# A decoder layer on one core: moments and normalisation of the next expert tokens placed in the group ahead, and routing in 20 steps

## The reference, cut to what matters

```python
scores = sigmoid(x @ gate_w.T);  scores_c = scores + correction_bias
group_scores = sum(top_k(scores_c.reshape(N, 4, 2), 2)[0], -1)
group_mask = one for the 2 best groups, else 0
scores_for_choice = where(repeat(group_mask, 2) > 0.5, scores_c, 0.0)
topk_idx = top_k(scores_for_choice, 4)[1]
topk_w = take_along_axis(scores, topk_idx);  topk_w = 2.5 * topk_w / (sum(topk_w) + 1e-20)
cw = topk_w scattered to the 8 experts
y_e = (silu(x @ Wg_e) * (x @ Wu_e)) @ Wd_e          # each expert, x is layernorm(x2)
out = x2 + sum_e cw_e * y_e + shared expert
```

## Time and profile before

| | |
|---|---|
| time, median of 3 runs (us) | 671.16 (670.51 to 671.90) |
| the profiled execution (us) | 671.73, of which the span is 669.9 |
| busy, share of the span | PE 97%, PEld 83%, DVE 72%, ACT 51%, POOL 37% |
| granted TensorE clock | 1.00 throughout, the 2.4 GHz level |
| expert stage | from 389.9 to 669.9, seven groups |

### The profile page before, as it was taken

How to read it: one execution, slowest core, us unless ns; L and a number is a source line. 1 busy time by engine, 2 the same in 40 slices (tenths; PEclk the granted TensorE clock), 3 DMA queues, 4 the chain that set the end, 5 groups by cost and what they waited for, 6 DMA issues and landing times. The chain is left out here.

```text
span 669.9 us, 11734 instructions
## 1 busy us (share of the span) xinstructions
PE 651.4 (97%) x3848; PEld 554.5 (83%) x3848; DVE 484.3 (72%) x1263; ACT 341.9 (51%) x794; POOL 248.7 (37%) x321
## 2 busy tenths in 40 slices
PE   5999999999999999999999989999999999999997
PEld 3868978888789788897887877888888888888887
DVE  5688778868788788787887978766767666667433
ACT  4555665667556666676576454343423434333321
POOL 2136365172463642624653132323233232332232
PEclk9999999999999999999999999999999999999999
DMA  7625134043150340522633180413204132140300
GB/s 203 168 57 156 36 101 139 0 136 102 53 158 27 107 131 0 159 79 63 189 93 100 49 269 1 158 64 127 94 3 159 60 126 94 28 162 1 135 24 32
DMA packets 51806, 64.44 MB, mean 96 GB/s; under 512 B 3944, under 2 KB 49560, under 8 KB 50880
## 3 DMA queue, kind: packets, MB, share of 16 engines
q1 hardware_dynamic: 51776, 64.06, 31.4%
HBM read 56.60 MB, written 7.45 MB: 96 GB/s over the span
## 5 line engine op out<-in xcount | busy, mean ns | idle before, releaser
L1593 POOL TENSOR_TENSOR xt<-xt,cw_wide 128x512 f32<-128x512 f32 x55 | 73.4, 1334 | 173.9 <-ACT xt L1550 173.9
L1617 DVE TENSOR_TENSOR res<-bank,xt 128x512 f32<-128x512 f32 x62 | 42.6, 687 | 53.1 <-POOL xt L1593 47.4
L1554 ACT ACTIVATE a_hi<-res 128x512 fp32r<-128x512 f32 x42 | 26.6, 634 | 86.5 <-DVE res L1617 86.5
L75 PE MATMUL bank<-h_hi,w_lo 128*128 128x512 f32 x168 | 67.4, 401 | 0.1
L77 PE MATMUL bank<-h_hi,w_hi 128*128 128x512 f32 x168 | 66.1, 393 | 0.0
L76 PE MATMUL bank<-h_lo,w_hi 128*128 128x512 f32 x168 | 66.0, 393 | 0.0
L75 PE MATMUL bank<-w_hi,op_lo 128*128 128x256 f32 x184 | 53.3, 290 | 0.5 <-DVE op_lo L1130 0.5
L76 PE MATMUL bank<-w_lo,op_hi 128*128 128x256 f32 x184 | 51.4, 280 | 0.0
L77 PE MATMUL bank<-w_hi,op_hi 128*128 128x256 f32 x184 | 51.4, 279 | 0.0
L1007 POOL TENSOR_TENSOR wz_lo<-tmp,wz_hi 128x512 fp32r<-128x512 f32 x28 | 35.0, 1281 | 37.6 <-DVE tmp L1173 37.6
L1622 DVE TENSOR_TENSOR a_lo<-res,a_hi 128x512 fp32r<-128x512 f32 x42 | 32.6, 776 | 22.4 <-ACT a_hi L1554 22.4
(11 more groups left out here) (239 smaller groups left out, 2059.8 us busy)
## 6 DMA issues: line engine op xcount, KB each, us to landing
cw_wide<-in_ctx_t SPq DMA_DIRECT2D x32, 375.0 KB
ctxf<-in_ctx SPq DMA_DIRECT2D x32, 375.0 KB
cw_wide<-cw_scratch SPq DMA_DIRECT2D x7, 1536.0 KB, 7.8
xt<-in_x SPq DMA_DIRECT2D x8, 448.0 KB, 4.1
x_scratch<-x2b SPq DMA_DIRECT2D x8, 448.0 KB, 3.2
x2n<-x_scratch SPq DMA_DIRECT2D x7, 512.0 KB, 4.7
cw_wide<-cw_scratch SPq DMA_DIRECT2D x7, 512.0 KB, 4.4
x2t<-x_scratch SPq DMA_DIRECT2D x7, 512.0 KB, 4.0
```

The source lines that it names most:

```text
L75: pe.matmul(dst, a_lo, b_hi, start=first, stop=False, **kw)
L1554: act.activation(a_hi[n % (AHEAD + 1)][:, :], af[(p + n) % 2][:, :], ACT.Copy).then_inc(a_hi_ok, 1)
L1593: pool.tensor_tensor(sg[b][:, :], sg[b][:, :], cw_wide[p][:, ORDER[n], :], ALU.mult).then_inc(sgw_ok, 1)
L1617: dve.tensor_tensor(af[b][:, :], u_bank[b][:, :], sg[b][:, :], ALU.mult).then_inc(af_ok, 1)
```

## The change

The change does two things.

**The norm moves ahead by most of a group.** `moments3`, `rstd3` and `normalise3` for group g + 2 now stand in group g: on DVE the moments after `act_low` 6 and the normalisation after `act_low` 7, on POOL rstd3 between expert 6 and expert 7. They are gone from the start of a group. Groups 0 to 4 do this (`more`).

**Routing in 20 steps.** Three pairs of a comparison or scaling and a product become one scalar_tensor_tensor each: choice, wsel and cw. The tile gmask is gone.

```diff
-            step(dve.tensor_scalar(gmask[:, :, :], grank[:, :, :], 2.0, None, ALU.is_lt))
-            step(dve.tensor_tensor(choice[:, :, :].rearrange("p t (a b) -> p t a b", b=2), halves,
-                                   gmask[:, :, :].unsqueeze(3).to_broadcast([P, T, 4, 2]), ALU.mult))
+            step(dve.scalar_tensor_tensor(choice[:, :, :].rearrange("p t (a b) -> p t a b", b=2),
+                                          grank[:, :, :].unsqueeze(3).to_broadcast([P, T, 4, 2]), 2.0, halves, ALU.is_lt, ALU.mult))
...
-            step(dve.tensor_scalar(erank[:, :, :], erank[:, :, :], 4.0, None, ALU.is_lt))
-            step(dve.tensor_tensor(wsel[:, :, :], score[:, :, :], erank[:, :, :], ALU.mult))
+            step(dve.scalar_tensor_tensor(wsel[:, :, :], erank[:, :, :], 4.0, score[:, :, :], ALU.is_lt, ALU.mult))
...
-            step(dve.tensor_tensor(wsel[:, :, :], wsel[:, :, :], winv[:, :].unsqueeze(2).to_broadcast([P, T, NEXP]), ALU.mult))
-            step(dve.tensor_scalar(cw[:, :, :], wsel[:, :, :], EXPERT_SCALE, None, ALU.mult))
+            step(dve.scalar_tensor_tensor(cw[:, :, :], winv[:, :].unsqueeze(2).to_broadcast([P, T, NEXP]), EXPERT_SCALE, wsel[:, :, :],
+                                          ALU.mult, ALU.mult))
...
@@ POOL, group @@
-                    if not last and not is_first(g):
-                        rstd3(pool, g + 1)
                     for n in range(2 if is_first(g) else 1, NE):
                         expert(g, p, n)
+                        if n == 6 and more:
+                            rstd3(pool, g + 2)
@@ DVE, group @@
-                    if not last and not is_first(g):
-                        moments3(dve, g + 1)
...
-                            if n == 0 and not is_first(g):
-                                normalise3(dve, g + 1)
                         if not is_first(g) or n >= 1:
                             act_low(g, p, n)
+                        if n == 6 and more:
+                            moments3(dve, g + 2)
+                        if n == 7 and more:
+                            normalise3(dve, g + 2)
```

More of the change, by code:

```diff
@@ L124, in decoder_layer @@
         lg, den, score, scorec, choice, wsel, cw = (osb(n, [P, T, NEXP]) for n in ("lg", "den", "score", "scorec", "choice", "wsel", "cw"))
-        gsum, grank, gmask = (osb(n, [P, T, 4]) for n in ("gsum", "grank", "gmask"))
+        gsum, grank = (osb(n, [P, T, 4]) for n in ("gsum", "grank"))
         g_gt, g_eq = osb("g_gt", [P, T, 4, 4]), osb("g_eq", [P, T, 4, 4])
@@ L144, in decoder_layer @@
         sg_ok, sgw_ok, af_ok, a_hi_ok, a_lo_ok = osem("silu_ready"), osem("silu_weighted"), osem("act_ready"), osem("act_hi"), osem("act_lo")
-        ROUTE_STEPS = 23
+        ROUTE_STEPS = 20
         ORDER = [NEXP] + list(range(NEXP))
@@ L273, in route_groups @@
             step(dve.reduce_sum(grank[:, :, :], g_gt[:, :, :, :], AX))
-            step(dve.tensor_scalar(gmask[:, :, :], grank[:, :, :], 2.0, None, ALU.is_lt))
-            step(dve.tensor_tensor(choice[:, :, :].rearrange("p t (a b) -> p t a b", b=2), halves,
-                                   gmask[:, :, :].unsqueeze(3).to_broadcast([P, T, 4, 2]), ALU.mult))
+            step(dve.scalar_tensor_tensor(choice[:, :, :].rearrange("p t (a b) -> p t a b", b=2),
+                                          grank[:, :, :].unsqueeze(3).to_broadcast([P, T, 4, 2]), 2.0, halves, ALU.is_lt, ALU.mult))
         def route_ranks(dve, g):
-            step = stepper(dve, g, 11)
+            step = stepper(dve, g, 10)
             mine, other = pairs(choice[:, :, :], 8, 3), pairs(choice[:, :, :], 8, 2)
@@ L288, in route_weights @@
         def route_weights(dve, g):
-            step = stepper(dve, g, 15)
+            step = stepper(dve, g, 14)
             step(dve.reduce_sum(erank[:, :, :], e_gt[:, :, :, :], AX))
-            step(dve.tensor_scalar(erank[:, :, :], erank[:, :, :], 4.0, None, ALU.is_lt))
-            step(dve.tensor_tensor(wsel[:, :, :], score[:, :, :], erank[:, :, :], ALU.mult))
+            step(dve.scalar_tensor_tensor(wsel[:, :, :], erank[:, :, :], 4.0, score[:, :, :], ALU.is_lt, ALU.mult))
             step(dve.reduce_sum(wsum[:, :], wsel[:, :, :], AX))
@@ L1593, in expert, with group @@
                     pool.tensor_tensor(sg[b][:, :], sg[b][:, :], cw_wide[p][:, ORDER[n], :], ALU.mult).then_inc(sgw_ok, 1)
-                def group(g, p, last):
-                    if not last and not is_first(g):
-                        rstd3(pool, g + 1)
+                def group(g, p, more):
                     for n in range(2 if is_first(g) else 1, NE):
                         expert(g, p, n)
-                group(0, 0, False)
+                        if n == 6 and more:
+                            rstd3(pool, g + 2)
+                group(0, 0, True)
                 with pool.Fori(0, NG2 // 2 - 1) as it:
-                    group(2 * it + 1, 1, False)
-                    group(2 * it + 2, 0, False)
+                    group(2 * it + 1, 1, True)
+                    group(2 * it + 2, 0, True)
                 group(NG2 - 2, 1, False)
-                group(NG2 - 1, 0, True)
+                group(NG2 - 1, 0, False)
             @block.vector
@@ L1634, in split_low, with group @@
                     dve.tensor_tensor(w_lo[e][:, :], w_f[e][:, :], f32(w_hi[e][:, :]), ALU.subtract).then_inc(e_lo_ok, 1)
-                def group(g, p, nth, last):
-                    if not last and not is_first(g):
-                        moments3(dve, g + 1)
+                def group(g, p, nth, last, more):
                     late = 1 if is_first(g) else 0
@@ L1666, in _ @@
                 dve.tensor_tensor(w2_lo[:, :], w_staged[0][:, :], f32(w2_hi[:, :]), ALU.subtract).then_inc(e_lo_ok, 1)
-                group(0, 0, None, False)
+                group(0, 0, None, False, True)
                 with dve.Fori(0, NG2 // 2 - 1) as it:
-                    group(2 * it + 1, 1, it + 1, False)
-                    group(2 * it + 2, 0, it + 1, False)
-                group(NG2 - 2, 1, NG2 // 2, False)
-                group(NG2 - 1, 0, NG2 // 2, True)
+                    group(2 * it + 1, 1, it + 1, False, True)
+                    group(2 * it + 2, 0, it + 1, False, True)
+                group(NG2 - 2, 1, NG2 // 2, False, False)
+                group(NG2 - 1, 0, NG2 // 2, True, False)
                 finish(NG2 - 1, 0, NG2 // 2 + 1)
```

## The result

The changed kernel takes 674.58 us (median of 6 runs, 672.13 to 675.73) against 671.34 us before (6 runs, 669.96 to 671.91). The ratio is 1.0054, with a 95% interval of 1.0033 to 1.0076: slower by 2.2 to 5.1 us. The forecast was 674.5 us, slower. The profiled execution has a span of 671.9 us (before 669.9).

The account below looks back on a forecast made before the run. PE, busy 97% of the span, was taken to bound the kernel, so any new stand is paid in full. Losses of 6.4 us less gains of 3.1 us add 3.3 us to 671.16: 674.5 us, range 671.4 to 676.8 us.

Parts of the forecast that it names:

- Part 1: Attention stage: three routing steps fewer on DVE ahead of the last products gain 0.65 us; bounds 0.4 and 0.66.
- Rival D: Attention stage and group 0's cw: the shorter routing's gains don't come; 675.8 us at most, a variant of the forecast.
- Part 2: Group 0, transposes of cw: PE goes on 0.66 us earlier with the shorter routing; 0.3 us of idle time stays.
- Part 3: Groups 1 to 4: the shorter routing gains nothing by itself, but `product` 6 comes 0.66 us earlier against PE.
- Part 4: Start of groups 1 and 2: moving the norm removes PE's stands of 1.10 and 0.72 us; gain 1.8 us.
- Part 5: First matmuls of groups 1 to 5: POOL's wait for the moments delays expert 7 and `product` 7; stands sum to 5.9 us.
- Part 6: PE's `gate_up` 1: normalisation ahead of `product` 8 makes a stand of 0.1 us in each of five groups, 0.5 in all.
- The lock: Routing beside POOL's expert 6: the new wsel sits out the rest of it, as L292 did (822 ns against 182).
- rival A: Routing in groups 1 to 4: wsel isn't held up by POOL; stands 3.3 us in all, 671.4 us, chance 13%.
- Rival B: Ahead of `product` 8: one normalisation instruction precedes POOL's expert 8; up to 0.35 us more per group, 676.2 us, chance 15%.
- Rival C: Group starts: `product` 7 isn't late for PE, POOL's wait costs nothing, only gains are left; 668.0 us, chance 5%.

Follow-up runs that it names:

- experiment 3: The changed kernel with the 23 old routing steps, that is, the move of the norm alone: 679.42 us, ratio to before 1.0130.
- experiment 2: The kernel before with the 20 routing steps alone, the norm staying at the start of the group: 668.35 us, ratio to before 0.9959.
- experiment 1: The changed kernel with POOL's rstd3 behind expert 7 instead of ahead of it, DVE's order untouched: 667.42 us, ratio to before 0.9936.
- experiment 4: The changed kernel with rstd3 behind expert 7 in group 0 alone, groups 1 to 4 as changed: 670.60 us, ratio to before 0.9997.
- experiment 7: The changed kernel with rstd3 behind expert 7 in groups 1 to 4, ahead of it in group 0 only: 669.68 us, ratio to before 0.9987.
- experiment 8: The changed kernel with POOL's power computed twice, the first into a tile that nobody reads: 680.68 us, ratio to before 1.0142.

## Why the prediction was right, point by point

**Part 1** (0.65 us in the attention stage). From the first matmul of the attention part to the first of the expert stage the traces have 367.35 and 367.45 us with 23 steps (before, experiment 3) and 366.75 to 367.02 with 20 (the ten others). That is about 0.5 us, within the bounds, and PE's wait for wz_lo went from 0.43 to under 0.2 us. Rival D is out. The stage itself began at 387.28 rather than near 389.25, since this execution had the early start.

**Part 2** (0.66 us at the cw transposes). The gap there went from 1.13 to 0.73 us, so it gave 0.4, over a third less. `product` 6 did come 0.57 us sooner behind the first matmul of the stage (25.75 before, 25.18 after), but PE, out of the slow even groups, came 0.16 us sooner as well.

**Part 3** (the short routing gains nothing by itself in groups 1 to 4). This step failed in two groups. By itself it takes 0.7 us off the stand ahead of the h3 transposes of group 2, which the working had put down to the move, and 0.1 off a wait in group 4 that is not shown as idle time. Its other half, `product` 6 coming 0.66 us earlier against PE, held: 5.94 us in group 1 of experiment 2 against 5.99 in the working.

**Part 4** (1.8 us from moving the norm). The stands went, as said. But 0.72 of it was due to the routing's chain and came without any move. The move, placed well, is worth 1.3 us of stage (experiment 2 against experiment 1, 277.6 and 276.4), nearly all of it the stand of group 1, or 0.9 us in the medians.

**Part 5** (POOL's wait; 2.35, 1.41, 0.63, 0.87 and 0.63, in sum 5.9). Measured 2.30, 0.88, 0.80, 0.88 and 0.80, in sum 5.7. The chain was 7.3 us instead of 7.4. In the new order PE comes 6.48 to 6.49 us behind `product` 6 in all of groups 1 to 4, where the working had 5.99, 6.77, 6.53 and 6.77. The traces show where both differences come from. In group 1 before, a routing step met POOL's expert and sat it out:

```profile
444.86 1.26 DVE L272 TENSOR_TENSOR g_gt<-g_gt,g_eq 128x64 f32<-128x64 f32 x1
```

In every other group that step took 0.23 us, and in the changed kernel in group 1 too. Ahead of it stood a gap of 0.29 us between two steps that no other group had. Experiments 2 and 3 have such a gap and the long step as well; where the gap comes from is not shown. The working carried this half microsecond over. And the 6.11 us of groups 2 and 4 held the 0.3 us of the slow even groups: 6.11 + 0.66 - 0.3 is 6.47. Experiments 1, 4, 7 and 8 showed the mechanism from three sides: the wait moved away, moved away by parts, and made longer.

**Part 6** (0.1 us ahead of `product` 8, five times). No wait is shown there. `product` 8 ended 11.58 us behind `product` 6 (11.65 in the working), but PE came 4.31 us after its late `gate_up` 0 rather than 4.17, since it restarts a little slowly (below), so it came at 467.07 and found it ready by a hair: in groups 2 to 5 `product` 8 ends 0.07 to 0.11 us ahead (in group 1, where the clock had slowed PE, 1.7). The first matmul of `gate_up` 1 is followed after 0.28 to 0.32 us in those four, where in experiment 1, with `product` 8 half a microsecond ahead or more, it is 0.23. So 0.05 to 0.09 us is lost here each time, 0.3 in all; by what, the trace doesn't say.

**The lock.** It held, so rival A is out: wsel took 0.83 us in the groups where it stands beside POOL's expert 6, and 0.19 in group 0 where POOL is idle; the choice step took 0.76 to 0.97 against 0.19. What the Trainium skill says (SBUF — State Buffer, section "Who interferes with whom") is borne out by this form with its two inputs in SBUF. Rival B did not happen: in all five groups the first of the four instructions started 0.08 or 0.09 us behind POOL's expert 8 and ended behind it, so POOL was not held up. The margin was as thin as the working said. Rival C of the prediction, the faster side, is out with every stand that was seen: POOL did not run expert 7 ahead of its wait.

**What wasn't in the sum.** The clock's fall behind the stand ahead of group 1, some 1.5 us in the executions that have it. The prediction took a stand to cost its length.

And the slow even groups, 1.2 us of the kernel before that the changed one doesn't have. Nothing in the prediction pointed at them.

The way and the mechanism were right. That the sum, 3.3 us, comes so near to the measured 3.2 is in part luck. For the expert stage alone the terms as measured are 5.7 (stands) + 0.9 (restarts at `gate_up` 0 and 1) + 1.6 (clock) - 1.8 (h3's stands) - 0.4 (cw) - 0.1 (group 4) - 1.2 (slow even groups) = 4.7 us, and the traces have 4.5. Less the 0.5 of the attention part that is 4.0 for the whole, which is what runs of like starts show (3.6 to 4.0). Restarts and clock, 2.5 us of loss, and the slow even groups, 1.2 us of gain, were all missing from the working, and the median of the changed kernel happens to lie between its two starts. By like starts, 11 of the 13 runs of the changed kernel have the time with the fall of the clock and two, 672.1 and 672.4 us, the time without it.

## What to carry to other kernels

A wait costs what is queued behind it on its own engine. Before a step with a wait inside is moved to an in-order engine that also hands on work that is due, put the handed-on work first; here two small POOL instructions one place later turned a loss of 3 us into a gain of 4. And a chain that runs through several engines is shortened at its head: three steps off the routing also took 0.7 us off a stand that seemed to belong to the norm. Before a gain is put down to an edit, set matmul against matmul in a part that the edit doesn't touch: here group 6, where neither the routing nor the norm stands, is 0.3 us quicker in some kernels, and with it go 1.2 us that this edit was not shown to have gained.

## What the hardware showed

- **The clock fell behind stands of about 2 us and more, in some executions only.** The first matmuls came at the half level (0.43 us from one of 512 columns to the next) behind stands of 2.30, 2.31, 1.99 and 3.26 us, and at full speed behind stands of 2.27 and 2.31 in other kernels. It did so too at the start of the expert stage in experiments 3 and 4 (granted clock 0.83 from 386 to 396), where PE had been idle for 1.7 and 1.9 us a little earlier, as it did in all kernels, most of them without the fall. Behind the stands of 2.3 and 1.99 us the price was some 1.6 us, behind that of 3.26 it was 2.8. What decides between the two was not found.
- **PE restarts with a loss of about 0.14 us.** Behind a stand at the full clock the first matmul of 512 columns is followed after 0.34 us, the later ones after 0.23 (420.25 and 420.59 in experiment 7), and the twelve of `gate_up` 0 take 2.88 us rather than 2.74 (419.48 to 422.22 in experiment 1).
- **Waits below some 0.15 us can't be seen as idle time.** A matmul that is shown with 0.28 us is followed by the next after 0.12; its shown end covers a wait of that size. Distances between the same places of two kernels show it; here one of 0.12 us in group 4 of the kernel before. They need care, since they also hold what is no wait (next point).
- **The same PE work can run 0.3 us slower in every second group of one kernel and not of another.** This was so in groups 0, 2, 4 and 6 of the kernel before and of experiments 3 and 8, at the full clock. In group 6, which takes 44 us, their matmuls of 512 columns came every 232.6 to 232.9 ns, in the nine other traces every 230.0 or 230.1. The instructions of PE in it are the same. The cause was not found.
- **A power of four elements a row takes POOL 1.01 us**, nearly as much as its multiplication of 512 elements a row (1.3 us).
